# Rounds of sums in the order in which their phases are complete, and two clears and loads further back in the queue, in a graph layer on one core

## What is computed

```python
h = jnp.maximum(_layernorm(x, axis=-1), 0.0)
row, col = (edge_index[0], edge_index[1])          # row = src, col = dst (sorted)
msg = jnp.concatenate([h[col], edge_attr], axis=1)
m = jax.nn.relu(msg @ W1a.T + b1a) @ W1b.T + b1b
sums = jax.ops.segment_sum(m, row, num_segments=n_nodes)
agg = sums / jnp.maximum(counts, 1.0)[:, None]
z = jax.nn.relu(jnp.concatenate([h, agg], axis=1) @ W2a.T + b2a) @ W2b.T + b2b
out = x + jnp.concatenate([z, h], axis=1) @ Wr.T + br
```

## The kernel before

| rounds after group | before | after the change |
|---|---|---|
| 16 to 31 | phase 0 (9 rounds) | the same |
| 36 | none | phase 1, 2 rounds |
| 39, 40, 41 | none | phase 1, 1 + 2 + 2 rounds |
| 42 | CH, 2 rounds | phase 1, 2 rounds (12 and 4 matmuls) |
| 43 to 47 | CH, 2 each | CH, 2 each |
| 48 | CH, phase 1 | CH, 2 rounds |
| 49 | phase 1, 2 rounds | CH, 1 round of 6 matmuls |
| 50, 51 | phase 1, 2 each | phase 2, 2 each |
| 52 | phase 1 (12 + 4 matmuls), phase 2 | phase 2, 2 rounds |
| 53 | phase 2, 1 round | phase 2, 3 rounds |
| left over | phase 2 (7 rounds), 3, 4 | phases 3, 4 |

## Time and profile before

### The profile page before, as it was taken

The page is one execution under the profiler, slowest core; times in us unless marked ns, Lnnn a source line. Parts: engine busy times, 40 slices in busy tenths (PEclk is TensorE's granted clock), DMA queues, the critical chain, the costliest instruction groups (busy, mean ns, idle before and its releaser), DMA issues.

```text
span 566.3 us, 9605 instructions
## 1 busy us (share of the span) xinstructions
PE 447.5 (79%) x3223; PEld 399.6 (71%) x3223; DVE 374.8 (66%) x1429; ACT 133.1 (24%) x239; POOL 366.2 (65%) x408
## 2 busy tenths in 40 slices
PE   6637459999999889888699845069987998887786
PEld 5536349888696887868597845078977987887774
DVE  7767266635767868575647632078787798988784
ACT  3332212313233231423133421102111120000064
POOL 4777776475577777777776777777777777730000
PEclk9677867957899999989899987569988899999888
DMA  8999956643848487877545877939989878976521
GB/s 184 322 308 243 284 159 169 171 146 89 274 133 285 118 261 227 255 222 240 168 133 164 249 202 251 302 121 342 327 269 323 266 257 279 304 218 191 133 69 58
DMA packets 62320, 123.46 MB, mean 218 GB/s; under 512 B 9369, under 2 KB 33374, under 8 KB 62270
## 3 DMA queue, kind: packets, MB, share of 16 engines
q1 hardware_dynamic: 49598, 91.25, 54.8%
q0 software_dynamic: 12672, 31.58, 17.0%
HBM read 71.53 MB, written 51.25 MB: 217 GB/s over the span
## 4 chain that ended last, share of the span: by engine, by line
POOL 37%; PE 27%; issue 15%; DVE 8%; DMA 7%; SPq 3%; ACT 1%; POOLq 0%; DVEq 0%
POOL slots_dram L557 27%; PE bank L1219 9%; POOL pairs_dram L540 9%; PE bank L1199 5%; DMA dstb<-in_dst 4%; DVE oh L746 4%; PE bank L1228 2%; PE bank L1250 2%; DMA rows<-slots_dram 2%; DMA slots_dram<-pay,pos_i 2%; PE bank L1163 1%; PE bank L1146 1%; SPq L403 1%; DVE eo L731 1%; PE bank L1314 1%
## 5 line engine op out<-in xcount | busy, mean ns | idle before, releaser
L557 POOL DMA_INDIRECT slots_dram<-pay,pos_i x300 | 296.9, 990 | 98.4 <-issue 89.6
L1219 PE MATMUL bank<-rows,oh 128*125 128x130 f32 x1100 | 146.9, 294 | 53.6 <-DVE oh L746 51.8
L1219 PEld LDWEIGHTS bank<-rows,oh 128*125 128x125 f32 x1100 | 138.6, 203 | 61.6 <-issue 59.5
L1199 PE MATMUL bank<-pw,eo 128*128 128x128 f32 x856 | 120.2, 300 | 9.5 <-DVE eo L731 7.4
L1199 PEld LDWEIGHTS bank<-pw,eo 128*128 128x128 f32 x856 | 113.8, 214 | 17.6 <-issue 15.9
L746 DVE TENSOR_SCALAR oh<-marks,rows 128x125 f32<-128x125 f32 x550 | 113.4, 290 | 3.5 <-DMA rows<-slots_dram 3.1
L540 POOL DMA_INDIRECT pairs_dram<-pay,pos_c x64 | 63.7, 995 | 36.2 <-DVE pos_c L723 18.5
L1017 ACT ACTIVATE pay<-bank 128x1024 f32<-128x1024 f32 (+1 forms) x37 | 37.5, 1013 | 196.0 <-PE bank L1199 178.9
L731 DVE TENSOR_SCALAR eo<-dstb,lane 64x256 f32<-64x256 int32 x214 | 67.3, 374 | 11.4 <-DMA dstb<-in_dst 10.5
L1228 PE MATMUL bank<-hid,xch 116*128 116x131 f32 (+1 forms) x512 | 64.1, 282 | 12.5 <-DVE xch L697 10.9
L1228 PEld LDWEIGHTS bank<-hid,xch 116*128 116x128 f32 (+1 forms) x512 | 61.3, 195 | 15.7 <-issue 13.2
(11 more groups left out here) (185 smaller groups left out, 364.3 us busy)
## 6 DMA issues: line engine op xcount, KB each, us to landing
rows<-slots_dram SPq DMA_DIRECT2D x24, 864.0 KB, 6.3
dstb<-in_dst SPq DMA_DIRECT2D x54, 256.0 KB
eo<-in_edges_T SPq DMA_DIRECT2D x54, 256.0 KB, 4.3
rows<-pairs_dram SPq DMA_DIRECT2D x12, 864.0 KB, 9.5
slots_dram<-zeros SPq DMA_DIRECT2D x9, 756.0 KB, 6.3
slots_dram<-pay,pos_i POOLq DMA_INDIRECT x300
rows<-slots_dram SPq DMA_DIRECT2D x8, 432.0 KB, 3.9
rows<-slots_dram SPq DMA_DIRECT2D x16, 216.0 KB, 2.7
```

The source lines that it names most:

```text
L557: pool.indirect_dma_start(out=slots_dram[:, :], out_offset=bass.IndirectOffsetOnAxis(ap=pos_i[:, u, k:k + 1], axis=0), in_=pay[:, u, k, :] ...
L1199: last = T.matmul(bank[:, 2 * (g % 2) + k // 4, (k % 4) * HID:(k % 4 + 1) * HID], eo[:, u, k * 128:(k + 1) * 128], pw[:, g % WB, a, :], st ...
L1219: last = T.matmul(o[0:BN, v * SW:(v + 1) * SW], oh2[:, r % 2, n, :], rows[:, sum_no[r] % RR, n, 0:SW], start=(t == 0), stop=(t == TB[ph] - ...
```

## The change

The diff, but for a line that only moves:

```diff
     PAIRS_BEFORE_CLEAR = 2
+    CLEAR_FROM = 6
...
+    AFTER_PHASE = [4, 4, 4, 2, 1, 0, 4]
     sum_rounds = []
-    for ph in [0, CH] + list(range(1, NPH)):
+    for ph in sorted(range(NPH + 1), key=lambda ph: END_GROUP[ph] + AFTER_PHASE[ph]):
         m = min(512 // SW, TPR // TB[ph])
...
             load_edges(5)
-            for p0, p1 in HALVES:
-                sp.dma_start(xr[p0:p1, :, :], x.rearrange("(i b) f -> i b f", b=NB)[p0:p1, :, :]).then_inc(s_xr, 16)
-
...
-                if g == 3:
+                if g == CLEAR_FROM:
                     sp.wait_ge(S["zero"], 2)
-                if 3 <= g < 3 + len(CLEAR_PIECES):
-                    clear_chunks(g - 3)
+                if CLEAR_FROM <= g < CLEAR_FROM + len(CLEAR_PIECES):
+                    clear_chunks(g - CLEAR_FROM)
+                if g == CLEAR_FROM + len(CLEAR_PIECES) - 1:
+                    for p0, p1 in HALVES:
+                        sp.dma_start(xr[p0:p1, :, :], x.rearrange("(i b) f -> i b f", b=NB)[p0:p1, :, :]).then_inc(s_xr, 16)
                 for r in after[g - 1]:
                     load_round(r)
```

## The result

The changed kernel takes 540.48 us (median of 4 executions, 535.59 to 547.29), the kernel before 565.35 us (4 executions, 558.52 to 565.9). The ratio is 0.9559, 95% interval 0.9495 to 0.9622: faster, by 24.9 us. The prediction said 544, between 535 and 555. Ratios leave out executions that fell in the slower of two states of a chip, and the profiled execution of the kernel before (568.35 us, 2.9 above the median) is itself a slow one.

A forecast was written before the change was run, and what follows sets the result against it. The prediction took the kernel as bound first by SP's queue, then PE and DVE, then POOL, and at the end DVE and PE. 7 - 1 + 15.7 = 21.7 us off the 565.45 median gave 544, range 535 to 555.

The forecast's parts named there:

- The front: Clears and `xr` moved behind later loads: group 7's one-hots start 7.1 us earlier, and POOL's end moves by the full 7.
- The lower bound of 5.8: Least gain at group 7's one-hots, with the lag of group 3's scatters unchanged: 71.89 - 66.1 = 5.8 us.
- about 11: Sign of being right: POOL's waits for `pos_c` fall from 18.5 us to about 11.
- near 494: Sign of being right: POOL's last scatter, at 500.76 us before, starts near 494.
- The price of the moved rounds: Two rounds after group 36 delay `pos_c` of group 37 some 6 to 9 us against 10.7 slack; charged 1, bounds 0 and 4.
- Rival D: SP's wait for scatters through group 31 blocks `dstb` and `eo` of group 38: slower, about 577 us; chance 0.06.
- The end: Behind positions of groups 52 and 53: 64 fewer matmuls, 5.33 rounds at 2.95, gain 15.7 us, bounds 11 and 18.7.
- the 5 us that the text set as a limit: Sign of being wrong: DVE waits for `rows` in the last 60 us for more than 5 us in all.
- The sum: Whole kernel: 7 - 1 + 15.7 = 21.7 us off, 544.6 in span, 543.75 from the median, stated as 544.
- Rivals A: Front: DVE waits for `xr` or slowed scatters instead, so moving clears and `xr` gives 0; result 551 us, chance 0.2.
- C: Front: scatters land soon, so moving clears and `xr` gains 12 us; result 539 us, chance 0.1.
- Rival B: Late rows hold PE, or small loads bind the end: rounds gain 7.5, front 5, 553 us (558 without front); chance 0.16.

The follow-up runs named there:

- e8: Changed kernel with message and sum matmuls contracting over 64 of 128 rows: 689.32 us in one execution, on a chip with the kernel before at 572.08 us.

## Why the prediction held, step by step

**The front, 7 us predicted, 6.5 measured at group 7 and 6.8 at POOL.** The one-hots of group 7 came 6.5 us earlier (65.41 against 71.89), held by the landing of group 3's scatters as the step said. The lag was mis-sized: I took 8.6 us from the chain at 422.90, it was 10.2 (54.91 to 65.12), as in the front before. The lower bound of 5.8 was worked out from that lag; that it came to 6.5 is the 0.8 us by which the scatter itself started earlier, and that is luck. By the rule of the Trainium skill, DMA: Bandwidth & Descriptors, Queues, rings and completion order, the scatters would gain nothing when SP's ring changes what it holds, and the trace agrees: 10.1 us before, 10.2 after. `xr` was hidden, first used at 83.49 with no wait. POOL gained 6.8 us between the end of group 3 and group 13 (from 0.8 to 7.6 ahead), which is the step as written. Its waits for `pos_c` fell to 10.6 us, "about 11" in the text, and its last scatter started at 494.08 ("near 494"). But that last agreement is in part luck: to the 7.6 us came 1.6 from one long scatter of the kernel before, and 2.5 were lost behind it. All this is seen only with both parts in: the clears alone never ran on a chip where POOL sets the pace.

**The price of the moved rounds, 1 us predicted, 2.5 measured.** POOL's wait at group 37 is 1.48 us, 1.18 above the gap of issue: that is the 1 us of the step. What it left out is groups 38 to 45, where the other moved rounds lie and POOL's scatters take 1.3 us longer in all with the DMA engines at 0.97. That the moved loads cause this is argued, not shown. Rival D, the queue blocked by SP's wait for the scatters through group 31, did not come.

**The end, 15.7 us predicted, 18.0 measured to the first tail round.** The count of 64 matmuls fewer, 5.33 rounds, was right, and as work of DVE it is 15.3 us (windows above). The term was 2.3 us short. What the step left out is that DVE also stood less: 10.4 us of 64.9 before, 7.7 of 46.9 now. Of these 2.7 us, 1.8 are waits for `rows` (3.1 us in three waits before, 0.34 and 0.96 now); 1.3 us behind group 53 stays under the 5 us that the text set as a limit, so the small loads beside scatters cost little.

**The tail, nothing predicted, 2.6 us measured.** The step treated everything from the first tail round on as a constant shift. Of the 2.6 us 1.2 belong to the stretch ahead of it, as said above, and 1.4 go with TensorE's granted clock (mean 0.87 before, 0.95 now). Whether the change brings this about is open, with one profile of each kernel; that PE was about as idle in both ahead of the place where only one clock fell speaks for chance.

**The sum.** 21.7 predicted, 26.5 between the two spans, 24.9 between the medians. The 26.5 are 5.8 + 18.0 + 2.6, and the 5.8, which stands for the predicted 7 - 1, has the long scatter and both losses of POOL in it. So the mechanism held. Within the front the errors cancelled, which is luck; the end and the tail, 2.3 and 2.6 us, both came out above the sum. Rivals A (the stall stays) and C (scatters land early) are out by the 65.41 and the 10.2. Rival B (moved rounds are not free) is out on this chip as to its size, by the 2.5 us and by the 18.0. On the other chips it is what happens, with more weight than I gave it: some 11 of the 21 us come back in the middle, the rounds alone give 8, and the changed kernel's ratio is 0.9982. The condition was in the text (the rounds lie in DVE's waits of 30.5 us). That it hangs on the chip was not.

## What to carry to other kernels

Order a list of deferred work by when it becomes possible, if something behind the head of the list could fill a hole of the engines that do it. Count what such a move is worth only behind the last point that another engine's pace sets, and only while that engine does set it. Then look at that engine's own instructions, one by one, for what the moved work does to them. When one stall in a queue is taken away, look first for the next wait at the same instruction and take its lag from the same stretch of the trace, since the same step cost 8.6 us elsewhere and 10.2 here.

## What was not expected of the hardware

With the contraction of 1,956 of the 3,223 listed matmuls halved, from 128 rows to 64, a kernel took 149 us more, in one execution and on another chip than the 540.48: the mean granted clock fell from 0.91 to 0.67 and PE's busy time rose from 441.6 to 641.3 us, with the same instructions and columns. The clock stayed at 0.50 while PE had no idle time. The Trainium skill, TensorE: Matmul & The Clock Gate, What's actually happening, says that the clock gate is set by how busy the array has been of late. Here the array is listed busy for 20.00 of 20 us, with half of its rows in use in most of the matmuls, at 1.2 GHz, and in the changed kernel for 18.36 of 20 us at 2.4. So in this trace the listed busy time and the granted clock don't go together. Why is not shown.

The same program takes 565 us on some chips and 748 on others, a difference seven times the effect of the change. In the slower ones TensorE takes 0.7 us or more for each listed matmul in stretches of 16 us. In the one shown the recorded clock is 0.50 from 203 us on. That is slower than the level of 1.2 GHz by itself, at which e8's stand 0.22 us apart (20 us by 91). What holds it is open.
